# Pairwise coefficients of a delta-rule scan: from TensorE, ScalarE and GpSimd to DMAs through DRAM, with the unknown kept in PSUM and beta applied to one column at a time

## The chip, the cores and the metric

The kernel runs on one core of one Trainium2 chip. The metric is the device time of one execution in microseconds (us), the median of the runs shown. A core has five engines that run side by side and meet at semaphores: TensorE (PE, matrix products, its weight loads are listed as PEld), VectorE (DVE), ScalarE (ACT), GpSimd (POOL), and SyncE (SP), which here only issues DMAs. Each engine works through its own list of instructions in order.

## The reference, cut to what matters

The input is `x` of 4 sequences x 2048 tokens x 512 features. A gated delta-rule attention with 16 heads of 32 features comes first, then a mixture of 16 expert columns, of which one is chosen for each token. The part that the change touches is the scan over time of the attention:

```python
def step(S, inp):
    k_t, q_t, v_t, beta_t, a_t = inp
    S = S * a_t[..., None, None]
    kv_mem = jnp.einsum('bhd,bhde->bhe', k_t, S)
    delta = (v_t - kv_mem) * beta_t
    S = S + k_t[..., :, None] * delta[..., None, :]
    y_t = jnp.einsum('bhd,bhde->bhe', q_t, S)
    return (S, y_t)
```

Here `beta_t` is a vector of 32 numbers for each head, and `a_t` one number.

## The kernel before

**The chunks.** The scan isn't run token by token. Time is cut into NT = 32 tiles of T = 64 tokens, a tile into NC = 2 chunks of C = 32 tokens, and a chunk into two halves of CS = 16 tokens. Inside a chunk the deltas obey a triangular system: delta of token t is beta(t) times (v(t) - what the state gives - the sum over earlier tokens s of A(s,t) x delta(s)), where A(s,t) is k(s).k(t) times a decay. There are four such halves to a tile, written (c, j): chunk c, half j. The 64 heads-times-sequences lie as 4 groups of 32 partitions (HP = 4) times G = 16 in the free dimension.

**One half.** `solve_half` (L1206 to L1235) runs on DVE. It forms v - `uk`, where `uk` is a PSUM bank that TensorE filled with what the state (and, for the second half, the first half) contributes, and multiplies it by beta into `U` in SBUF. Then, for each of 15 tokens t0, it multiplies the row of coefficients `pairs` of t0 by column t0 of `U` (L1227) and subtracts that from the later columns (L1230). Each of these operations is cut into two (`turns`, 8 of the 16 groups each), and an operation waits for the last but one before it (`behind=1`). At the end `U` is transposed into `delT` (L1234), which TensorE wants.

**The pairs.** The coefficient of a pair (s,t) must stand on all 32 partitions of its group, and be multiplied by beta(t) of each partition. TensorE spreads it with a selection matrix `sel` (`spread_pairs`, L417, 15 products for each half, in four packs through three shared PSUM banks `work`), ACT copies each pack to SBUF (`copy_pairs`, L760), and POOL multiplies in place by beta (`pairs_times_beta`, L1015, 15 operations for each half). Row t0 of `pairs` holds its later tokens contiguous.

**A step.** A step of the main loop handles three tiles at once: `chain` (the scan of one tile), `ahead` (norm, projections q, k, gate, beta, v, and decays of the next tile) and `after` (output norm, projection, and routing to a column for the tile before). On each engine the order is written out by hand in `step(...)`. DVE's is: solve (0,0); the transposes `kd` and `decay_products(1)`; the norm of outputs; solve (0,1); first statistics of y, `add_to_state`; solve (1,0); statistics of x1, gates; solve (1,1); `decay_products(0)` for the next tile; routing (`choose_columns`, L1287 on, `rows_of_tokens`); `add_to_state`. TensorE's products between two solves are `first_half_to_u` (L437, from (c,0) to (c,1)), or `change_state` (L459), `add_to_state` on DVE (L1242) and `state_to_u` (L429).

**Semaphores that the steps below name.** `vb_free` lets ACT overwrite beta and vT with those of the next tile; DVE gives it in solve (1,1), as soon as `U` is formed. A bank of `work` goes from use to use in the order of the table `TURNS`, modulo 3; the next use waits until the bank's reader is done, and that wait is seen at L365 on PE. `xfT`, `hid`, `logits` and `rank` are uses of the routing. SP loads tokens (L300), the residual (L307) and stores the output (L312), two DMAs each per step.

**The last stage.** Behind the 33 steps (to about 4.1 ms) a loop over 80 tiles of 128 gathered tokens computes the experts. It reads weights by DMA and isn't touched, but for the names of two buffers that it borrows.

## Time and profile before

| | |
|---|---|
| time of the runs | 4683.97 us median of 3 (4678.25 to 4697.39) |
| span of the profiled execution | 4724.7 us, which is also the span of the slowest (only) core |
| its TensorE clock | 0.871 of full speed, mean |
| PE, DVE, POOL, ACT busy in it | 80%, 66%, 41%, 33% |
| DMA | 173.32 MB, 37 GB/s over the span |

The profiled execution has no time of its own in the results beside the span; the span is 0.9% above the median of the three runs. Busy shares are averages over the main loop and the last stage, which have different limits. A matmul record's end is modelled, and a fp32 product shows as two records. In a timeline a row merges neighbouring instructions of one line; its columns are start, length, engine, line, operation, out<-in, shapes, count, and in brackets the idle time before it and what ended that.

### The profile page before, as it was taken

The page shows a single profiled execution, that of the slowest core. Times are in us where ns is not written, and L with a number is a line of the kernel's source. Part 1 is how long each engine was busy: PE and PEld are TensorE (multiplying, and loading weights), DVE is VectorE, ACT ScalarE, POOL GpSimd, SP SyncE. Part 2 cuts the span into 40 slices and gives each one's busy share as a digit, 9 for nine tenths or more (in the row PEclk, how much of TensorE's full clock was granted, in tenths as well). Part 3 has the DMA queues.
Part 4 walks back from the last instruction along what each step waited for, and adds up shares of the span by engine and source line. Part 5 has one row for each costly group of instructions (what it writes and reads, how often), then busy time and mean ns, then how long its engine had stood idle before and what let it go on. Part 6 is the DMA issues. An engine that isn't in the chain of part 4 may idle for free. (4 is left out here: it accounts for less than half of the span.)

```text
span 4724.7 us, 160369 instructions
## 1 busy us (share of the span) xinstructions
PE 3787.6 (80%) x63204; PEld 2988.3 (63%) x63204; DVE 3127.4 (66%) x12284; ACT 1547.3 (33%) x2631; POOL 1924.0 (41%) x3051
## 2 busy tenths in 40 slices
PE   5888888888898888888888888888888887455553
PEld 4676676666677666676677677666667776333332
DVE  1666767766666667666766677776667667556555
ACT  2333333333333333333333333333333332211110
POOL 1343333344333333333333333334433433157776
PEclk9988989888998989988988998988899988676776
DMA  2000000000000000000000000000000000166663
GB/s 92 11 20 21 18 18 21 20 21 20 18 19 20 20 14 18 21 20 21 20 21 20 20 17 19 21 20 21 20 21 16 20 20 16 53 162 150 144 150 84
DMA packets 129486, 173.32 MB, mean 37 GB/s; under 512 B 25425, under 2 KB 67025, under 8 KB 128097
## 3 DMA queue, kind: packets, MB, share of 16 engines
q1 hardware_dynamic: 112096, 129.30, 9.7%
q0 software_dynamic: 16640, 33.71, 3.4%
q8 instruction: 510, 8.36, 0.8%
q14 instruction: 240, 1.96, 0.1%
HBM read 107.99 MB, written 59.15 MB: 35 GB/s over the span
## 5 line engine op out<-in xcount | busy, mean ns | idle before, releaser
L374 PE MATMUL work<-xT,w_sb 128*128 128x256 f32 x5120 | 1399.2, 424 | 85.3 <-PEq L365 84.5
L1015 POOL TENSOR_TENSOR pairs<-pairs,beta 128x240 f32<-128x240 f32 (+14 forms) x1920 | 802.4, 455 | 1072.1 <-POOLq L1011 1072.1
L374 PEld LDWEIGHTS work<-xT,w_sb 128*128 128x128 f32 x5120 | 1036.7, 211 | 290.8 <-issue 138.3
L1227 DVE TENSOR_TENSOR Ut<-pairs,U 128x120 f32<-128x120 f32 (+14 forms) x3840 | 917.3, 276 | 4.7
L1230 DVE TENSOR_TENSOR U<-U,Ut 128x120 f32<-128x120 f32 (+14 forms) x3840 | 877.3, 266 | 0.0
L417 PE MATMUL work<-A,sel 128*128 128x240 f32 (+14 forms) x3840 | 643.4, 318 | 118.3 <-PEq L365 118.0
L417 PEld LDWEIGHTS work<-A,sel 128*128 128x128 f32 x3840 | 592.5, 204 | 149.5 <-issue 129.3
L760 ACT ACTIVATE pairs<-work 128x480 f32<-128x480 f32 x512 | 292.5, 571 | 437.6 <-ACTq L759 436.0
L1214 DVE TENSOR_TENSOR Ut<-vT,uk 128x128 f32<-128x128 f32 x256 | 62.1, 284 | 414.1 <-DVEq L1334 230.7
L1004 POOL TENSOR_TENSOR kqd<-kq,eg 128x1024 f32<-128x1024 f32 x64 | 150.9, 2357 | 342.0 <-POOLq L1071 342.0
L384 PE MATMUL work<-qsq,squares 128*128 128x512 f32 x256 | 163.4, 725 | 125.7 <-PEq L365 125.7
L437 PEld LDWEIGHTS uk<-A,delT 16*32 16x32 f32 x8192 | 109.1, 136 | 241.2 <-issue 241.2
L437 PE MATMUL uk<-A,delT 16*32 16x16 f32 x8192 | 121.3, 201 | 148.8 <-PEq L436 146.3
L783 ACT ACTIVATE qraw<-work 128x512 f32<-128x512 f32 x128 | 76.4, 597 | 496.7 <-ACTq L782 496.7
L491 PE MATMUL work<-wo_sb,ctxT 128*128 128x512 f32 x512 | 229.2, 601 | 4.3 <-PEq L365 4.3
L729 PE MATMUL kkq<-w_sb,kq 128*128 128x512 f32 x160 | 136.7, 952 | 102.2 <-PEq L728 102.2
L709 PE MATMUL work<-squares,w_sb 128*128 128x128 f32 x320 | 71.8, 371 | 165.6 <-PEq L707 162.5
L1081 POOL DMA_INDIRECT xs_rows<-xfw,slot x64 | 64.1, 1002 | 328.3 <-POOLq L1079 318.5
L1052 POOL TENSOR_TENSOR x<-x,y 128x512 f32<-128x512 f32 x64 | 81.5, 1273 | 271.6 <-POOLq L1051 271.6
L709 PEld LDWEIGHTS work<-squares,w_sb 128*128 128x128 f32 x320 | 52.2, 193 | 214.8 <-issue 214.7
L1030 POOL TENSOR_TENSOR kd<-kd,dec 128x512 f32<-128x512 f32 x64 | 68.7, 1074 | 275.2 <-POOLq L1028 269.4
L974 ACT ACTIVATE kq<-work 128x512 f32<-128x512 f32 x80 | 47.8, 597 | 389.3 <-ACTq L972 364.9
(193 smaller groups left out, 6006.4 us busy)
## 6 DMA issues: line engine op xcount, KB each, us to landing
w_sb<-xs_rows SPq DMA_DIRECT2D x80, 258.0 KB, 2.8
w_sb<-in_w_cols SPq DMA_DIRECT2D x80, 256.0 KB, 4.4
w_sb<-in_proj_w SPq DMA_DIRECT2D x80, 256.0 KB, 4.4
xt<-in_x SPq DMA_DIRECT2D x66, 256.0 KB, 3.7
x<-in_x SPq DMA_DIRECT2D x64, 256.0 KB, 3.7
out<-x SPq DMA_DIRECT2D x64, 256.0 KB, 3.3
w_sb<-in_w_in SPq DMA_DIRECT2D x1, 5120.0 KB, 17.6
xs_rows<-w_sb SPq DMA_DIRECT2D x17, 258.0 KB, 2.6
```

The lines of the kernel that those rows point to most:

```text
L374: mm = pe.matmul(w[:, half * BT:(half + 1) * BT], w_sb[:, f, j * D + hg * P:j * D + (hg + 1) * P], xT[:, f, :], start=(f == 0), stop=(f == ...
L384: pe.matmul(w, blk1, qsq[n % 2][:], start=True, stop=True).then_inc(s["ss_full"], 1)
L417: mm = pe.matmul(w[:, o:o + n], sel[:, j * CS + t0, :], A[c][:, :, 0, j * CS + t0 + 1:(j + 1) * CS], start=(o == 0), stop=True, skip_group ...
L437: on_tiles(half, "corr_full", lambda g, q, q_half: pe.matmul(uk[q, g, CS:C], delT[c][q_half, g, :], A[c][q_half, g, 0, CS:C], start=False, ...
L491: mm = pe.matmul(w, flat(ctxT[:, hg * B + tb * BL:hg * B + (tb + 1) * BL, :]), wo_sb[:, hg, :], start=(hg == 0), stop=(hg == KD - 1))
L709: mm = pe.transpose(m_tp[u % 2][:, f * P:(f + 1) * P], xs[u][:, f * P:(f + 1) * P], ident)
L729: pe.matmul(m_yp[u % 2], hm[u % 2], pw[u], start=True, stop=True).then_inc(s["m_y"], 1)
L760: link(nc.scalar.activation(pairs[j][:, OFF[pack[0]]:OFF[pack[0]] + n], bank("pair", c, j, i)[:, 0:n], ACT.Copy))
L1004: link(nc.gpsimd.tensor_tensor(kqd[c][:], kq[:, :, c], eg[:, :, c * C:(c + 1) * C].unsqueeze(2).to_broadcast([P, G, 2, C]), ALU.mult))
L1015: ins = nc.gpsimd.tensor_tensor(a, a, beta[:, :, t:t + WID[t0]], ALU.mult)
L1227: link(v.tensor_tensor(Ut[:, g, 0:n], pr[:, g], U[:, g, at:at + 1].to_broadcast([P, G // 2, n]), ALU.mult), behind=1)
L1230: link(v.tensor_tensor(U[:, g, at + 1:at + 1 + n], U[:, g, at + 1:at + 1 + n], Ut[:, g, 0:n], ALU.subtract), behind=1)
```

## The change

The row of coefficients is now broadcast by DMA. `decay_products` writes the k part of A alone, transposed to [time, group] (`Ak`), and the q part to `Aq`. SP writes `Ak` (256 KB) to a DRAM buffer, waits until it is there, and reads it back in 8 DMAs for each half, with each row repeated on the 32 partitions of its group: 4 of 32x8x256 and 4 of 32x8x128 elements, 1.5 MB for a half, 6 MB and 0.5 MB written for a step. `pairs` now has the group index innermost. TensorE's `spread_pairs`, ACT's `copy_pairs`, POOL's `pairs_times_beta` and the 2 MB constant `sel` are gone. `U` is gone too: DVE solves in place in the PSUM bank `uk`. The pairs no longer hold beta, so each column is multiplied by its beta just before it is used (`times_beta`, 16 times two small operations for each half), and `vb_free` is given at the end of solve (1,1) and not at its beginning. SP's list is reordered round the new DMAs.

```diff
-TURNS = [("pair", 0, 1, i) for i in range(len(PACKS))] + [
...
+PIECE = CS // 2
+PIECES = [(0, 0), (PIECE, PIECE)]
+TURNS = [
+    ("xT", 0), ("xT", 1), ("qk", 0), ("rms", 0), ("alpha",), ("qk", 1), ("rms", 1), ("ss", 0),
+    ("wo", 0), ("wo", 1), ("qk", 2), ("ss", 1), ("G", 0), ("G", 1), ("qk", 3),
+    ("ss", 2), ("gate", 0), ("ss", 3), ("gate", 1), ("beta", 0), ("xfT", 0), ("xfT", 1), ("beta", 1), ("hid",),
     ("v", 0), ("logits",), ("v", 1), ("rank",)]
...
+            def fetch_pairs(c):
+                sp.wait_ge(s["Ak_ready"], 1)
+                sp.sem_inc(s["Ak_ready"], -1)
+                sp.dma_start(pair_rows[c].rearrange("h s r -> (h s) r"), Ak[c][:].rearrange("p t g -> p (t g)")).then_inc(s["rows_out"], 16)
+                sp.wait_ge(s["rows_out"], 16)
+                sp.sem_inc(s["rows_out"], -16)
+                for j in range(2):
+                    sp.wait_ge(pairs_free[j], 1)
+                    sp.sem_inc(pairs_free[j], -1)
+                    for s0, t0 in PIECES:
+                        for h in range(HP):
+                            rows = pair_rows[c, h, j * CS + s0:j * CS + s0 + PIECE, (j * CS + t0) * G:(j + 1) * CS * G]
+                            sp.dma_start(pairs[j][DH * h:DH * h + DH, s0:s0 + PIECE, t0:CS, :].rearrange("p s t g -> p s (t g)"),
+                                         rows.unsqueeze(0).to_broadcast([DH, PIECE, (CS - t0) * G])).then_inc(pairs_in[j], 16)
...
-            with sp.Fori(0, NT - 2) as i:
-                load_tokens(i + 2)
-                add_and_store(i)
...
+            with sp.Fori(0, NT - 3) as i:
+                load_residual(i)
+                fetch_pairs(1)
+                load_tokens(i + 3)
+                store(i)
+                fetch_pairs(0)
...
             def first_half_to_u(c, half):
 
                 if not half:
+                    pe.wait_ge(s["A_ready"], 1)
+                    pe.sem_inc(s["A_ready"], -1)
                     pe.wait_ge(s["delT_ready"], 1)
                     pe.sem_inc(s["delT_ready"], -1)
                 on_tiles(half, "corr_full", lambda g, q, q_half: pe.matmul(
-                    uk[q, g, CS:C], delT[c][q_half, g, :], A[c][q_half, g, 0, CS:C],
+                    uk[q, g, CS:C], delT[c][q_half, g, :], Ak[c][q_half, CS:C, g],
                     start=False, stop=True, skip_group_check=True))
...
-                link(v.tensor_tensor(A[c][:], kkq[:], dec[:, :, c * C:(c + 1) * C].unsqueeze(2).to_broadcast([P, G, 2, C]), ALU.mult))
+                d = dec[:, :, c * C:(c + 1) * C]
+                link(v.tensor_tensor(Ak[c][:].rearrange("p t g -> p g t"), kkq[:, :, 0, :], d, ALU.mult))
+                dve.sem_inc(s["Ak_ready"], 1)
+                link(v.tensor_tensor(Aq[c][:], kkq[:, :, 1, :], d, ALU.mult))
...
                 for g in turns:
-                    link(v.tensor_tensor(Ut[:, g], vT[:, g, th], uk[:, g, h], ALU.subtract), behind=1)
-                for g in turns:
-                    link(v.tensor_tensor(U[:, g, h], Ut[:, g], beta[:, g, th], ALU.mult), behind=1)
-                dve.wait_ge(s["pr_ready"], 1)
...
+                    link(v.tensor_tensor(uk[:, g, h], vT[:, g, th], uk[:, g, h], ALU.subtract), behind=1)
...
+                dve.wait_ge(pairs_in[j], 16 * HP * len(PIECES))
...
+                def times_beta(t0):
+                    at, t = j * CS + t0, c * C + j * CS + t0
+                    for g in turns:
+                        link(v.tensor_tensor(uk[:, g, at:at + 1], uk[:, g, at:at + 1], beta[:, g, t:t + 1], ALU.mult), behind=1)
 
                 for t0 in range(CS - 1):
                     n, at = WID[t0], j * CS + t0
-                    pr = pairs[j][:, OFF[t0]:OFF[t0] + G * n].rearrange("p (g t) -> p g t", g=G)
+                    times_beta(t0)
+                    pr = pairs[j][:, t0, t0 + 1:CS, :].rearrange("p t g -> p g t")
                     for g in turns:
-                        link(v.tensor_tensor(Ut[:, g, 0:n], pr[:, g], U[:, g, at:at + 1].to_broadcast([P, G // 2, n]),
+                        link(v.tensor_tensor(Ut[:, g, 0:n], pr[:, g], uk[:, g, at:at + 1].to_broadcast([P, G // 2, n]),
...
+                times_beta(CS - 1)
                 dve.wait_ge(dve_step, link.n)
-                dve.sem_inc(s["pairs_free"], 1)
-                link(v.transpose(delT[c][:], U[:]))
+                dve.sem_inc(pairs_free[j], 1)
+                if (c, j) == (NC - 1, 1):
+                    dve.sem_inc(s["vb_free"], 1)
+                link(v.transpose(delT[c][:], uk[:]))
```

On VectorE, the beginning of solve (0,1) in the first chain step read before (line, operation, out<-in, shape, repeats):

```order
L1214 TENSOR_TENSOR Ut<-vT,uk 128x128 x2
L1216 TENSOR_TENSOR U<-Ut,beta 128x8x16 x2
L1227 TENSOR_TENSOR Ut<-pairs,U 128x8x15 x2
L1230 TENSOR_TENSOR U<-U,Ut 128x8x15 x2
L1227 TENSOR_TENSOR Ut<-pairs,U 128x8x14 x2
L1230 TENSOR_TENSOR U<-U,Ut 128x8x14 x2
```

At the same place in the changed kernel (its line numbers differ):

```order
L1182 TENSOR_TENSOR uk<-vT,uk 128x8x16 x2
L1192 TENSOR_TENSOR uk<-uk,beta 128x8 x2
L1199 TENSOR_TENSOR Ut<-pairs,uk 128x8x15 x2
L1202 TENSOR_TENSOR uk<-uk,Ut 128x8x15 x2
L1192 TENSOR_TENSOR uk<-uk,beta 128x8 x2
L1199 TENSOR_TENSOR Ut<-pairs,uk 128x8x14 x2
L1202 TENSOR_TENSOR uk<-uk,Ut 128x8x14 x2
```

The multiplication of the whole half by beta has gone, and a pair of 128x8 operations stands ahead of every pair of products; each link of the chain now has `uk`, in PSUM, among its operands.

On TensorE, the end of a step and the beginning of the next read before (`su` is `change_state`, `uk` is `state_to_u`):

```order
L459 MATMUL su<-delT,kd 32x32 x32
L417 MATMUL work<-A,sel 128x240
L417 MATMUL work<-A,sel 128x224
L417 MATMUL work<-A,sel 128x16
L417 MATMUL work<-A,sel 128x208
L417 MATMUL work<-A,sel 128x192
L417 MATMUL work<-A,sel 128x80
L417 MATMUL work<-A,sel 128x176
L417 MATMUL work<-A,sel 128x160
L417 MATMUL work<-A,sel 128x144
L429 MATMUL uk<-kqd,S 32x32 x32
```

The same place now:

```order
L548 MATMUL work<-oh,squares 128x16 x2
L478 MATMUL su<-delT,kd 32x32 x32
L446 MATMUL uk<-kqd,S 32x32 x64
L420 MATMUL work<-squares,xn 128x128 x4
L469 MATMUL uq<-Aq,delT 32x32 x32
```

`state_to_u` follows `change_state` at once; the three packs of spread pairs ahead of it, and the fourth between its halves, have gone.

## Rows read from the trace of the kernel before

**Rows 1.** The page: busy time, share of the span, instructions.
```profile
PE 3787.6 (80%) x63204; PEld 2988.3 (63%) x63204; DVE 3127.4 (66%) x12284; ACT 1547.3 (33%) x2631; POOL 1924.0 (41%) x3051
```
**Rows 2.** Timeline of DVE: first solve, last step's first solve, last transpose.
```profile
116.32 0.49 DVE L1214 TENSOR_TENSOR Ut<-vT,uk 128x128 f32<-128x128 f32 x2 [15.64 <-DVEq L1334]
...
3961.55 0.48 DVE L1214 TENSOR_TENSOR Ut<-vT,uk 128x128 f32<-128x128 f32 x2 [5.57 <-DVEq L1334]
...
4039.99 0.71 DVE L1234 STREAM_TRANSPOSE delT<-U 128x512 f32<-128x512 f32 x1 [0.51 <-DVE U L1230]
```
**Rows 3.** Groups by line: busy, mean ns, idle before, releasers.
```profile
L1227 DVE TENSOR_TENSOR Ut<-pairs,U 128x120 f32<-128x120 f32 (+14 forms) x3840 | 917.3, 276 | 4.7
L417 PE MATMUL work<-A,sel 128*128 128x240 f32 (+14 forms) x3840 | 643.4, 318 | 118.3 <-PEq L365 118.0
...
L1214 DVE TENSOR_TENSOR Ut<-vT,uk 128x128 f32<-128x128 f32 x256 | 62.1, 284 | 414.1 <-DVEq L1334 230.7 <-DVEq L1349 131.4 <-DVEq L1376 40.9
```
**Rows 4.** Timeline of DVE and POOL, a solve beside POOL's multiplications.
```profile
2030.36 1.27 DVE L1227 TENSOR_TENSOR Ut<-pairs,U 128x80 f32<-128x80 f32 x2
...
2030.14 6.20 POOL L1015 TENSOR_TENSOR pairs<-pairs,beta 128x240 f32<-128x240 f32 x15 [2.23 <-POOLq L1011]
```
**Rows 5.** Timeline of DVE, a solve with POOL idle.
```profile
2050.25 0.48 DVE L1214 TENSOR_TENSOR Ut<-vT,uk 128x128 f32<-128x128 f32 x2 [0.35 <-DVEq L1395]
...
2051.29 0.48 DVE L1227 TENSOR_TENSOR Ut<-pairs,U 128x120 f32<-128x120 f32 x2
...
2059.34 0.30 DVE L1227 TENSOR_TENSOR Ut<-pairs,U 128x8 f32<-128x8 f32 x2
2059.55 0.29 DVE L1230 TENSOR_TENSOR U<-U,Ut 128x8 f32<-128x8 f32 x2
2059.98 0.71 DVE L1234 STREAM_TRANSPOSE delT<-U 128x512 f32<-128x512 f32 x1
```
**Rows 6.** Groups that compare places of operands and strides.
```profile
L1317 DVE TENSOR_TENSOR lt<-work,base 128x32 f32<-128x32 f32 x32 | 6.1, 191 | 7.6 <-DVEq L1315 7.6
L1321 DVE TENSOR_TENSOR lt<-lt,col 128x32 f32<-128x32 f32 x32 | 6.1, 191 | 4.7
...
L1463 DVE TENSOR_REDUCE A<-sel 128x80 f32<-128x1280 f32 x3 | 6.9, 2294 | 0.1
L1462 DVE TENSOR_TENSOR sel<-sel,col 128x1280 f32<-128x1280 f32 x2 | 3.0, 1492 | 0.1
...
L824 ACT ACTIVATE qr<-qr 128x512 f32<-128x512 f32 x64 | 40.3, 630 | 7.5
L834 ACT ACTIVATE vT<-work 128x512 f32<-128x512 f32 x64 | 38.2, 597 | 214.3 <-ACTq L833 214.3
```
**Rows 7.** Timeline of PE (and one row of ACT), two steps' meeting.
```profile
2061.58 3.69 PE L499 MATMUL work<-xn,gw_sb 128*128 128x256 f32 x16
...
2066.67 0.98 ACT L929 ACTIVATE ctxT<-work,gb_sb 128x256 f32<-128x256 f32 x2
...
2078.82 1.99 PE L374 MATMUL work<-xT,w_sb 128*128 128x256 f32 x8
...
2111.83 2.04 PE L384 MATMUL work<-qsq,squares 128*128 128x512 f32 x2 [4.21 <-PEq L365]
...
2114.78 3.78 PE L374 MATMUL work<-xT,w_sb 128*128 128x256 f32 x8
```
**Rows 8.** Timeline of DVE, from the state to the next solve.
```profile
2085.25 0.69 DVE L1242 TENSOR_TENSOR S<-Sd,su 128x512 f32<-128x512 f32 x1 [0.37 <-DVEq L1241]
2091.92 0.48 DVE L1214 TENSOR_TENSOR Ut<-vT,uk 128x128 f32<-128x128 f32 x2 [5.98 <-DVEq L1334]
```
**Rows 9.** DMA: queue, issues with KB and us to landing; start of DVE.
```profile
q1 hardware_dynamic: 112096, 129.30, 9.7%
...
out<-x SPq DMA_DIRECT2D x64, 256.0 KB, 3.3
...
30.83 0.48 DVE L1414 MEMSET U<- 128x512 f32 x1 [30.83 <-DMA nw<-in_norm_w]
```

More of the change, by code:

```diff
@@ L252, in sandwich_kernel @@
         m_xs, m_wc = ([sem(f"{n}{u}") for u in range(MQ)] for n in ("m_xs", "m_wc"))
+        pairs_free, pairs_in = ([sem(f"{n}{j}") for j in range(2)] for n in ("pairs_free", "pairs_in"))
         work_free = [sem(f"work{i}_free") for i in range(NW)]
@@ L751, in norm_tokens @@
                     act.sem_inc(ready, 1)
-            def copy_pairs(c, j):
-                act.wait_ge(s["pairs_free"], 1)
-                act.sem_inc(s["pairs_free"], -1)
-                for i, pack in enumerate(PACKS):
-                    n = G * sum(WID[t0] for t0 in pack)
-                    act.wait_ge(s["pair_full"], 1)
-                    act.sem_inc(s["pair_full"], -1)
-                    link(nc.scalar.activation(pairs[j][:, OFF[pack[0]]:OFF[pack[0]] + n], bank("pair", c, j, i)[:, 0:n], ACT.Copy))
-                    act.sem_inc(bank_free("pair", c, j, i), 1)
-                act.sem_inc(s["pr_copied"], 1)
             def copy_outputs(c):
@@ L1096, in _ @@
                 pool.sem_inc(f, 1)
[L1097 to L1098 removed]
+            pool.sem_inc(s["qraw_free"], 2)
+            for free in pairs_free:
+                pool.sem_inc(free, 1)
             link.restart()
```

109 lines of the change are left out of this document (29 added, 80 removed).

## The prediction

> **What bounds the kernel now.** The page comes first: PE is busy for 80% of the span, DVE for 66%, POOL for 41% [rows 1]. That would make PE the bound, but the order of the work says more. I read DVE's timeline step by step. Solve (0,0) starts 32 times, first at 116.32 and last at 3961.55 [rows 2], so a step takes (3961.55 - 116.32) / 31 = 124.0 us. The four solves of a step hang on one another through the state, and everything else of DVE stands between them. From the start of a solve (L1214) to its transpose (L1234) I find, as means over the 32 steps (128 solves, the last transpose at 4039.99 [rows 2]), 14.3 us for (0,0), 12.3 for (0,1), 16.4 for (1,0) and 9.7 for (1,1), together 52.7. The gaps behind them are 11.9, 15.3, 10.6 and 33.2 us, 71.0 together (0.3 of rounding and edges). In the gaps DVE waits for PE, but little beyond the last one: 230.7 us over 32 steps, 7.2 for each, ahead of (0,0), 4.1 ahead of (0,1), 1.3 ahead of (1,0) [rows 3]. So the step is a chain that goes from DVE to PE and back, and the change is worth what it does to the four solves and the four gaps.
>
> **The solves now.** They do the same work and yet differ by 7 us. The reader sees why where POOL multiplies the pairs: beside its 6.20 us of L1015 a DVE pair at 128x80 takes 1.27 us [rows 4], where with POOL idle one at 128x120 takes 0.48 [rows 5]. Over all its sizes L1227 takes 276 ns in the mean, nearly what L1214 takes (284), which is larger than any of them [rows 3]. The undisturbed solve runs from 2050.25 to 2059.98, 9.73 us [rows 5]. Four of these would be 38.9: 13.8 us of each step are this collision.
>
> **The solve after.** POOL's multiplications go, and DVE's operations have only one operand in SBUF beside the PSUM one. L1214, which has that form, keeps a mean of 284 ns over 256 instances [rows 3], as when nothing is beside it (0.48 for two that overlap [rows 5]). So I start from 9.73 us and take the collision as gone. Then:
> - The product with beta over the half goes: the opening two pairs and a wait take 2051.29 - 2050.25 = 1.04 us [rows 5], one pair of them 0.4: -0.4.
> - 16 pairs of 128x8 operations with beta come in, each a link that the next one waits for. The smallest links now follow at 2059.55 - 2059.34 = 0.21 us [rows 5]: 16 x 0.21 = +3.4.
> - `pairs` is read with 64 bytes from token to token. The trace has one such case: a reduction of 1280 elements read across rows takes 2294 ns, an operation on the same 1280 in order 1492 [rows 6], 0.63 ns more for each element. In the larger half of the 15 links a link costs its throughput (two operations of 120 to 64 elements, 736 for the sum of the eight sizes), so 736 x 2 x 0.63 = 0.93; in the smaller ones only one operation's latency counts, 224 x 0.63 = 0.14. Together +1.1; the other bound is 0.
> - `uk` in PSUM is read and written by every link. A DVE operation that reads PSUM takes 191 ns as one that doesn't [rows 6]. No row shows DVE writing PSUM. The nearest is ACT, where the place of an operand moves an operation by 630 - 597 = 33 ns [rows 6]. So 46 links x 33 ns = 1.5 us for a solve, up or down; I take 0, since DVE's own rows show no difference.
>
> That gives 9.73 - 0.4 + 3.4 + 1.1 = 13.8 us, with bounds of 11.2 (no stride cost, PSUM faster) and 15.3. Four solves: 55.2 against 52.7, **+2.5** for a step.
>
> The rule on strides stands in the Trainium skill too ("SBUF — State Buffer", section "Door 1: The DMA port swizzle", the note on cachelines): reads that go to a new 16-byte line each time pay a penalty. The reduction's row agrees. It gives no figure, and the sum goes by the row.
>
> **The gaps after.** (0,0) to (0,1): `decay_products(1)` becomes two operations, one more fixed part of about 0.1, and the k part is written with a stride (0 to 0.63 x 512 = 0.3): +0.3. PE isn't nearer, since it waits here for DVE's `alpha`, behind it on that list: 4.21 us idle, then at the low clock [rows 7]. **+0.3.**
>
> (0,1) to (1,0): now PE's list is full; spread pairs go from it, 643.4 / 128 = 5.0 us for each half [rows 3]. But then DVE's own work decides, which adds up to 10 us to the end of `add_to_state` (operation by operation in its timeline, of which no row is shown), and behind it PE needs 3.6 us for `state_to_u` with its projection between the halves: 13.7. And the sum of squares 1 waits for the bank that DVE frees only after its first y: that way I count 15.8 when PE is at the low clock. Between them 14.8: **-0.5.**
>
> (1,0) to (1,1): DVE's own work throughout, 10.9 in most steps: **0 to +0.3**, I take +0.2.
>
> (1,1) to (0,0): spread pairs go in front of `state_to_u`. Now 2085.94 (end of the state) to 2091.92 is 6.0 us [rows 8]; 128 small products at the low clock take 2.1 and a hop 0.2, so 2.3 is left. Over all steps the wait shrinks from 7.2 to 2.4: -4.8. But `vb_free`, until now given 0.9 us into the solve, comes at its end, 13.7 us in. Queued behind ACT's beta(0) are the copies of `xfT`, and on PE behind its bank beta(1), the outputs, `gate_hidden`, v, logits, `change_state` and `ranks`; DVE waits for those. Before, PE was past them and started `gate_hidden` 1.6 us after the transpose began (2061.58 against 2059.98 [rows 5, 7]). After, counted from the transpose: ACT and two hops 0.9, beta(1) first half at the low clock 3.8 [rows 7], outputs 1.0, second half 2.0 [rows 7], outputs 0.7, so `gate_hidden` starts at 8.3 (6.7 later). Three packs of pairs behind it go (5.0), but then the GELU, which they hid, is in the way: the hidden layer ends at 2065.3 and the GELUs at 2067.65 [rows 7], with a hop 2.6 us, against 2.0 for v's first product, so 0.7 more. The logits come 2.5 us later than now, and with them the end of the state: 28.5 us after the transpose, where it is 2085.94 - 2059.98 = 26.0 [rows 5, 8]. With 4.8 gone and 2.6 come, **-2.2.**
>
> **The DMAs.** A solve's rows are 2048 packets. The hardware queue's mean packet costs 9.7% x 16 x 4724.7 / 112096 = 65 ns of an engine [rows 9], so 2048 x 65 / 16 = 8.4 us; writing `Ak` is like a store, 3.3 us [rows 9]. From `Ak` (2 us after the transpose) the rows for (0,0) are there at about 2 + 3.5 + 2 + 8.4 = 16 us, and DVE wants them at 31; those for (0,1) at 25, wanted at 57. Those of chunk 1 have more. So I cost them at nothing, hidden by the gap of 31 us; uncovered they would cost 14 us a step. SP's list holds token loads behind the second `pairs_free`, but `xt_free` comes later still, so nothing moves. PE, ACT and POOL lose about 20, 9 and 25 us of work a step, worth nothing beyond what is said.
>
> **Once.** `sel`, 2 MB of the 10 that are loaded before DVE starts at 30.83 [rows 9], goes. At the rate of those loads (10.4 MB within some 28 us) that is -5 us.
>
> **The sum.** A step: +2.5 + 0.3 - 0.5 + 0.2 - 2.2 = +0.3 us. 32 steps: +10; once: -5; the last stage 0. So +5 on the span of 4724.7, which is 0.9% above the median of the runs; on that median, **4688 us**: no change, as large terms cancel. A difference under 0.5%, 23 us or 0.7 us a step, is about what can't be told from none here.
>
> **Rivals.**
> 1. *The stride costs nothing and the small links overlap* (or PSUM is the faster place). For it: only a reduction shows the stride's cost, no product does. 1.1 us less for a solve, 4.4 for a step: 4688 - 141 = 4547. With PSUM at its lower bound too, 4353. Chance 0.28.
> 2. *Each link through PSUM is slower.* At the upper bound of 33 ns, 6.1 us a step: 4688 + 194 = 4882. It decides from 4 ns a link on. Against it: reading costs nothing in two DVE rows. Chance 0.17. The Trainium skill ("VectorE: DVE Perf Modes", section on the TRN2 errata) has a table by which an operation with its source in PSUM takes 120 cycles where one in SBUF takes 58, at 0.96 GHz 65 ns more. By that the kernel would be near 5070. The two 191 ns rows disagree with it for reads; whether writes behave so, no row shows.
> 3. *The late `vb_free` starves PE.* If PE stays at the low clock through the whole chain behind beta(1), each of its five projections of 2.0 takes 3.8: up to 9 us, I'd say half, 4.5 a step, +144: 4832. For it: after 4.21 us idle PE ran a projection in 3.78 [rows 7]. It decides as soon as a second projection is slow. Chance 0.15.
> 4. *The rows come late.* From 25 us for a solve's rows, three times my count, DVE waits at `pairs_in`; 10 us a step would be 5000. 1.5 MB for half a solve's gap leaves much room. Chance 0.06.
>
> My forecast itself has 0.34, with a range of its own of 4620 to 4760 (a solve within 0.5 us). Faster by over 0.5%: rival 1 and a share of the forecast, 0.38. Within 0.5%: 0.2. Slower: 0.42. Low end 4520, near rival 1; the high end of 4890 takes in rival 2 at its row bound and leaves out rival 4 and the skill's figure.
>
> **What the profile after would show.** A solve of 13.8 us in all four places, with no stretched pairs; pairs of 128x8 following at 0.21; a pair of L1199 at 128x120 of 0.63 us if the stride costs, where L1227's is 0.48 [rows 5], and one of L1202 of 0.48 if PSUM doesn't. The wait ahead of (0,0) near 2.4 us, and PE idle ahead of beta(1) for 5 to 6 us, then cold. POOL busy some 1100 us, DVE above 3100. No wait at `pairs_in`. I'm wrong if a solve lies outside 13 to 14.5, or the last gap outside 30 to 32.

## The result, and the profile after

The changed kernel takes 4760.84 us (median of 4 runs, 4743.73 to 4771.22) where the kernel before, run beside it, took 4681.11 (4674.5 to 4697.39, 4 runs): a ratio of **1.0157**, 95% interval 1.0129 to 1.0185. It is slower by 1.6%, inside the forecast range, on the side that I gave 0.42, and 73 us above the predicted 4688. The narrower range that I gave my own forecast ended at 4760, just below it.

The experiments, on three chips, gave the kernel before 4701, 4724, 4728 and 4727 us, so below everything goes by the ratio to the runs of before that were taken beside them. The kernel after was run beside one set alone, the one with the lowest time of before. Whether it moves as the kernel before does from set to set isn't known, so a difference from after of less than about 1% (4728 to 4681) isn't safe, though each ratio's own interval is within 0.3% of it. The given profile of before was long for that kernel (span 4724.7); one more (label e0_before) has 4699.5.

The page of after: busy time, and two DMA queues with their packets, MB and share of the 16 engines' span.

```profile
span 4741.9 us, 153635 instructions
PE 3372.4 (71%) x59364; PEld 2518.9 (53%) x59364; DVE 3181.5 (67%) x16187; ACT 1253.7 (26%) x2119; POOL 1114.3 (23%) x1131
...
q1 hardware_dynamic: 399696, 345.37, 34.1%
...
q8 instruction: 492, 8.06, 0.8%
```

PE lost 9 points of its share and POOL 18 [rows 1], and the time rose: neither was the bound. TensorE's mean granted clock is 0.814, where it was 0.871. The groups of after:

```profile
L1199 DVE TENSOR_TENSOR Ut<-pairs,uk 128x120 f32<-128x120 f32 (+14 forms) x3840 | 827.6, 254 | 0.0
L1202 DVE TENSOR_TENSOR uk<-uk,Ut 128x120 f32<-128x120 f32 (+14 forms) x3840 | 705.4, 225 | 0.0
L1192 DVE TENSOR_TENSOR uk<-uk,beta 128x8 f32<-128x8 f32 x4096 | 606.1, 171 | 5.1 <-DVEq L1187 2.4
...
L1182 DVE TENSOR_TENSOR uk<-vT,uk 128x128 f32<-128x128 f32 x256 | 63.3, 293 | 303.7 <-DVEq L1309 123.0 <-DVEq L1324 111.5 <-DVEq L1351 58.0
```

The wait for the rows (L1187) is 2.4 us in the whole kernel, all of it in the first solve: rival 4 is out. The wait ahead of (0,0) is 123.0 us, 3.8 a step, where before had 7.2 [rows 3] and I wanted 2.4. DVE's timeline at one solve (0,0):

```profile
2099.31 0.49 DVE L1182 TENSOR_TENSOR uk<-vT,uk 128x128 f32<-128x128 f32 x2 [2.50 <-DVEq L1309]
2099.89 0.25 DVE L1192 TENSOR_TENSOR uk<-uk,beta 128x8 f32<-128x8 f32 x2
2100.10 0.62 DVE L1199 TENSOR_TENSOR Ut<-pairs,uk 128x120 f32<-128x120 f32 x2
2100.65 0.46 DVE L1202 TENSOR_TENSOR uk<-uk,Ut 128x120 f32<-128x120 f32 x2
2101.02 0.29 DVE L1192 TENSOR_TENSOR uk<-uk,beta 128x8 f32<-128x8 f32 x2
```

These are the promised signs: beta's pair with the next link 0.21 behind it, 0.62 for the pair that reads `pairs` with a stride, 0.46 for the one in PSUM. The other side of the step is PE's timeline, from the transpose of (1,1) to the product of the state. Here is a step whose last transpose starts at 2190.54:

```profile
2191.44 3.75 PE L402 MATMUL work<-xT,w_sb 128*128 128x256 f32 x8 [8.05 <-PEq L393]
...
2198.81 1.53 PE L518 MATMUL work<-xn,gw_sb 128*128 128x256 f32 x6 [0.16 <-PEq L393]
...
2215.00 0.75 PE L478 MATMUL su<-delT,kd 32*32 32x32 f32 x64
2219.68 0.53 PE L446 MATMUL uk<-kqd,S 32*32 32x32 f32 x22 [3.92 <-PEq L445]
2222.32 1.70 PE L446 MATMUL uk<-kqd,S 32*32 32x32 f32 x106 [2.11 <-issue]
```

The first four rows are nearly as worked out: PE idle ahead of beta(1) (8 us, not 5 to 6), then at the low clock (granted 0.50), `gate_hidden` at 8.3 us after the transpose. The last row isn't: after 22 of the 128 records of `state_to_u(0)` (a product shows as two) PE stands for 2.11 us with nothing to wait for ("issue"). The solve starts 33.6 us after the transpose, not 31.0.

The step by parts, in us. A line's sum differs from its step by up to 0.6, since the parts average over the first and last steps as well. "Stalls" is PE's idle time put to its own issue, over the whole run (the sum in the view of waits). The expectations quote 170 and 238 us, from a coarser count.

| kernel | solves | gaps | step | stalls | ratio to before |
|---|---|---|---|---|---|
| before, given profile | 14.3, 12.3, 16.4, 9.7 | 11.9, 15.3, 10.6, 33.2 | 124.0 | 34 | 1 |
| e0_before | 14.9, 12.3, 16.3, 9.7 | 12.0, 15.4, 10.6, 31.6 | 123.3 | 25 | 1.0001 |
| **after** | 13.6, 13.4, 13.4, 13.5 | 11.8, 15.4, 10.6, 33.3 | 125.5 | 169 | 1.0157 |
| e1_two_betas | 13.8, 13.4, 13.4, 13.7 | 11.5, 16.4, 10.7, 26.7 | 120.0 | 233 | 0.9728 |
| e2_eighth_dma | 13.5, 13.4, 13.4, 13.5 | 11.5, 15.3, 10.6, 33.9 | 125.6 | 83 | 1.0101 |
| e3_no_beta | 10.3, 10.2, 10.1, 10.2 | 10.8, 17.7, 10.6, 33.4 | 113.7 | 247 | 0.9284 |
| e4_in_order | 12.6, 12.4, 12.4, 12.5 | 10.6, 16.0, 10.6, 33.9 | 121.4 | 240 | 0.9796 |
| e5_U_in_sbuf | 16.1, 13.5, 15.8, 13.6 | 12.6, 15.9, 10.6, 34.3 | 132.8 | 171 | 1.0532 |
| e6_before_no_mul | 10.4, 11.3, 12.4, 9.7 | 9.1, 16.0, 10.6, 33.4 | 113.3 | 38 | 0.9261 |
| e7_split | 13.7, 13.4, 13.4, 13.7 | 11.9, 16.5, 10.6, 27.9 | 121.5 | 142 | 0.9785 |
| e8_betas_eighth | 13.5, 13.4, 13.4, 13.7 | 11.7, 14.8, 10.6, 23.9 | 115.4 | 108 | 0.9387 |
| e9_unrolled | 13.6, 13.4, 13.4, 13.5 | 12.0, 16.1, 10.7, 34.2 | 127.3 | 229 | 1.0143 |
| e10_rows_in_order | 12.8, 12.4, 12.4, 12.7 | 10.6, 17.8, 10.6, 29.6 | 119.3 | 410 | 0.9627 |
| e12_loop_end_moved | 12.9, 12.4, 12.4, 12.7 | 11.0, 18.2, 11.4, 26.9 | 118.2 | 471 | 0.9548 |

### The profile page after: what moved, and what is told of

The parts are those of the page before. It is cut to its first block and busy times, and to the rows that moved or that the text cites. A ratio compares the mean times of both kernels' runs of the same rounds, so it can differ in the third digit from the quotient of the medians.

```text
span 4741.9 us, 153635 instructions
## 1 busy us (share of the span) xinstructions
PE 3372.4 (71%) x59364; PEld 2518.9 (53%) x59364; DVE 3181.5 (67%) x16187; ACT 1253.7 (26%) x2119; POOL 1114.3 (23%) x1131
## 3 DMA queue, kind: packets, MB, share of 16 engines
q1 hardware_dynamic: 399696, 345.37, 34.1%
q8 instruction: 492, 8.06, 0.8%
## 5 line engine op out<-in xcount | busy, mean ns | idle before, releaser
L402 PE MATMUL work<-xT,w_sb 128*128 128x256 f32 x5120 | 1482.6, 443 | 354.9 <-PEq L393 329.2
L1199 DVE TENSOR_TENSOR Ut<-pairs,uk 128x120 f32<-128x120 f32 (+14 forms) x3840 | 827.6, 254 | 0.0
L1202 DVE TENSOR_TENSOR uk<-uk,Ut 128x120 f32<-128x120 f32 (+14 forms) x3840 | 705.4, 225 | 0.0
L1192 DVE TENSOR_TENSOR uk<-uk,beta 128x8 f32<-128x8 f32 x4096 | 606.1, 171 | 5.1 <-DVEq L1187 2.4
L1182 DVE TENSOR_TENSOR uk<-vT,uk 128x128 f32<-128x128 f32 x256 | 63.3, 293 | 303.7 <-DVEq L1309 123.0
L446 PE MATMUL uk<-kqd,S 32*32 32x32 f32 x8192 | 119.6, 215 | 161.7 <-PEq L445 121.0
L456 PEld LDWEIGHTS uk<-Ak,delT 16*32 16x32 f32 x8192 | 101.4, 127 | 211.3 <-issue 211.3
L446 PEld LDWEIGHTS uk<-kqd,S 32*32 32x32 f32 x8192 | 106.0, 127 | 189.8 <-issue 188.9
L456 PE MATMUL uk<-Ak,delT 16*32 16x16 f32 x8192 | 113.7, 197 | 127.1 <-PEq L455 127.0
L510 PEld LDWEIGHTS work<-wo_sb,ctxT 128*128 128x128 f32 x512 | 105.7, 213 | 136.0 <-issue 133.4
```

What stands on the lines that cost most here:

```text
L402: mm = pe.matmul(w[:, half * BT:(half + 1) * BT], w_sb[:, f, j * D + hg * P:j * D + (hg + 1) * P], xT[:, f, :], start=(f == 0), stop=(f == ...
L446: on_tiles(half, "uk_full", lambda g, q, q_half: pe.matmul(uk[q, g], S[q, g, :], kqd[c][q, g, 0, :], start=(g == 0), stop=True, skip_group ...
L456: on_tiles(half, "corr_full", lambda g, q, q_half: pe.matmul(uk[q, g, CS:C], delT[c][q_half, g, :], Ak[c][q_half, CS:C, g], start=False, s ...
L510: mm = pe.matmul(w, flat(ctxT[:, hg * B + tb * BL:hg * B + (tb + 1) * BL, :]), wo_sb[:, hg, :], start=(hg == 0), stop=(hg == KD - 1))
L1192: link(v.tensor_tensor(uk[:, g, at:at + 1], uk[:, g, at:at + 1], beta[:, g, t:t + 1], ALU.mult), behind=1)
L1199: link(v.tensor_tensor(Ut[:, g, 0:n], pr[:, g], uk[:, g, at:at + 1].to_broadcast([P, G // 2, n]), ALU.mult), behind=1)
```

## The experiments

**The solve, term by term.** e0_before is the kernel before again, for a second profile.

> The kernel before, unchanged, for a second profile of it. The profiled execution of before had a span of 4724.7 us where its runs took about 4681; the one of the changed kernel was its fastest run. Both theories expect a ratio of 1.00 and a span near 4680; if the span is again near 4720, profiling costs this kernel something that it doesn't cost the changed one.

Measured: ratio 1.0001 (0.9988 to 1.0014), span 4699.5, a step of 123.3 us. The last gap is 31.6 us, where the given profile had 33.2: 1.5 us of the base that I counted from were that one execution's.

> The changed kernel without the multiplications of columns by beta, which leaves beta out of the result. It prices the 16 added links. If a link of two 128x8 operations costs 0.21 us, a solve falls from 13.4 by 3.4 to 10.1 us, and a step by up to 13.4: time about 4760 - 32 x 11 = 4400, a bit less gained in the gap behind (0,1), which PE shares. The rival (links of small operations overlap, and PSUM costs the difference) expects a fall of under 2 us a solve.

```
-                    times_beta(t0)
...
-                times_beta(CS - 1)
```

Measured: ratio 0.9284 (0.9267 to 0.9301). All solves take 10.1 to 10.3 us: the 16 links of beta cost 3.3 us, where I had 3.4. They are 13 us of every step, the largest single price in the kernel.

> The kernel after, but each of the 15 products of a solve reads its rows from pairs in the order in which they lie (the same number of elements, another order of them, so the pairing of values is not the reference's). It prices the stride alone. If reading 64 bytes from token to token costs 0.6 ns an element, as the reduction of the trace before said and as the 0.61 us of the first pair of L1199 says against 0.48, a solve goes from 13.4 us to 12.4 to 12.5, the first pair to 0.48, and the kernel from 4761 to about 4640 (1.0 us x 4 solves x 31). If the stride costs nothing and the longer pair has another cause, the solve stays at 13.4 and the kernel at 4760. If the stride costs but the chain elsewhere takes it up (PE), the solve shortens and the time falls by under half of it.

```
-                    pr = pairs[j][:, t0, t0 + 1:CS, :].rearrange("p t g -> p g t")
+                    pr = (the same elements of pairs[j], taken as (g, t) in the order in which they lie)
```

Measured: ratio 0.9796 (0.9773 to 0.982), solves of 12.4 to 12.6 us. L1199 falls from a mean of 254 ns to 217:

```profile
L1199 DVE TENSOR_TENSOR Ut<-pairs,uk 128x120 f32<-128x120 f32 (+14 forms) x3840 | 691.1, 217 | 0.0
```

The stride costs 1.0 us of a solve; I had 1.1. So the stride isn't free.

> The kernel after, but with the unknown in SBUF again (a buffer U, as before), everything else as after. If the place of the unknown costs nothing by itself, the solves stay at 13.4 us and the kernel between 4740 and 4780, except where POOL works in SBUF beside a solve: there operations with two operands in SBUF can be stretched, as beside L1015 in the kernel before; POOL's remaining 1114 us mostly lie in the gaps, so I expect 0 to 1 us more for one or two of the four solves, 0 to 120 us. If PSUM costs 33 ns for each of 46 links, a solve falls to 11.9 us and the kernel to about 4580. If PSUM made it faster by itself, all four solves grow alike.

```
-                    link(v.tensor_tensor(uk[:, g, h], vT[:, g, th], uk[:, g, h], ALU.subtract), behind=1)
+                    link(v.tensor_tensor(U[:, g, h], vT[:, g, th], uk[:, g, h], ALU.subtract), behind=1)
... (and so for the products with beta, the links and the transpose)
```

Measured: ratio 1.0532 (1.0507 to 1.0557), 3.7% slower than after, more than the 120 us (2.5%) that I expected at worst. The timeline says why: (0,1) and (1,1) still take 13.5 us, as with the unknown in PSUM, so PSUM by itself costs and gives nothing that shows. But (0,0) and (1,0) take 16. Here POOL's and DVE's rows at the start of one (0,0):

```profile
1145.77 1.05 POOL L982 TENSOR_TENSOR Sd<-S,eg_end 128x512 f32<-128x512 f32 x1 [2.35 <-POOLq L981]
1145.89 1.04 DVE L1193 TENSOR_TENSOR U<-U,beta 128x8 f32<-128x8 f32 x2
...
1146.78 2.37 POOL L987 TENSOR_TENSOR kqd<-kq,eg 128x1024 f32<-128x1024 f32 x1
...
1146.89 2.67 DVE L1200 TENSOR_TENSOR Ut<-pairs,U 128x120 f32<-128x120 f32 x2
```

A pair of 0.62 us takes 2.67, 0.3 more than POOL's product beside it, and beta's of 0.25 takes 1.04. With one operand in PSUM no L1199 of after is above 0.37 us. The Trainium skill ("SBUF — State Buffer", section "SBUF: two separate sides") states this as an exclusive lock on a port pair between GpSimd and a VectorE operation with two operands in SBUF, held for the whole instruction; by that rule DVE's pair can't end before POOL's product has, and the trace agrees: 1149.56 us against 1149.15.

> The kernel before without POOL's 15 products of a half's pairs with beta (beta is left out of the coupling of the pairs; PE's spread, ACT's copies and all else stay). It prices the collision of POOL with DVE alone. If POOL's products are what made the solves unequal, all four take 9.7 us, 38.9 for a step in place of 53.3, and the solves give 14 us a step; if DVE's chain still set the end the kernel would take about 4240. PE's list is still full (80% busy before, about 118 us a step at the clocks that it got), so I expect it to give back part of this in the gaps: 4350 to 4500, a step of 112 to 117 us. If POOL was not the cause, the solves stay unequal and the time near 4680.

```
-                for t0 in range(CS - 1):
-                    ... ins = nc.gpsimd.tensor_tensor(a, a, beta[:, :, t:t + WID[t0]], ALU.mult)
-                ins.then_inc(s["pr_ready"], 1)
+                pool.sem_inc(s["pr_ready"], 1)
```

Measured: ratio 0.9261 (0.9237 to 0.9285). The solves sum to 43.8 us, not to 38.9: POOL's products of pairs made 9.5 us of the collision against e0_before, and the 4.9 that are left fall where POOL's other products run: beside (0,0) the decay of k and q, beside (0,1) the gate, beside (1,0) the decays of the state; beside (1,1) POOL runs nothing, and it takes 9.7 us. My "13.8 us are this collision" was nearly right in sum and wrong in whom it named. The change takes away both, the first by dropping the products, the second by moving the unknown to PSUM.

**The last gap.**

> The changed kernel with two buffers for beta, used in turn; the semaphore vb_free, which now only guards vT, is given after the first two operations of solve (1,1), and ACT waits for it ahead of vT and not ahead of beta. Theory 1 (the loss is the late release of beta): PE's idle time of 8.1 us ahead of the second beta projection goes, and the gap from solve (1,1) to (0,0) falls from 33.3 us by 5 to 7: 4760 - 32 x 6 = about 4570, below both kernels. Theory 2 (the gap is set by what PE does behind that, or by PE's instructions coming late): the gap falls by less than 2 us, the time stays above 4700.

```
-        beta = sb("beta", [P, G, T])
+        beta = [sb(f"beta{p}", [P, G, T]) for p in range(2)]
... (ACT writes beta[1 - p] without a wait; vb_free, now for vT alone, is given at the solve's start)
```

Measured: ratio **0.9728** (0.9708 to 0.9748), 4.2% faster than after and 2.7% than before. The last gap falls by 6.6 us, near the 6.7 by which I had put `gate_hidden` later. So the late `vb_free` has its full price once the packs no longer stand beside it.

> The changed kernel, each read of pairs fetching one row of its eight: the same 16 DMAs a chunk with an eighth of the bytes and packets. What isn't fetched stays zero (a memset of pairs on POOL before the first step), so the pair terms of most tokens are left out. Theory 2: within runs of small products PE waited 170 us for nothing that the profile shows (issue), where before it was 34; if that is PE's instructions fetched behind the pair rows on the same 16 DMA engines, the 170 fall below 50 and the time falls by 40 to 110 us, to 4650 to 4720. Theory 1 (the loss is in the order of the semaphores): nothing changes, 4745 to 4775. Solves stay at 13.4 us in both.

```
-                            rows = pair_rows[c, h, j * CS + s0:j * CS + s0 + PIECE, ...]
+                            rows = pair_rows[c, h, j * CS + s0:j * CS + s0 + 1, ...]
```

Measured: ratio 1.0101 (1.0082 to 1.012). PE's stalls fall from 169 to 83 us, not below 50, and the time by only 0.55%, which is within the 1% that isn't safe. The last gap is even 0.6 us longer: in 28 of 31 steps a second projection behind the transpose runs near the low clock (granted 0.53):

```profile
2208.05 3.54 PE L402 MATMUL work<-xT,w_sb 128*128 128x256 f32 x8
```

After has this in 10 of 31 steps (su later by 2.3 us). Why it comes in some steps and not in others I can't say: the idle time ahead of beta(1) is 7.0 to 9.4 us in both kernels.

> The kernel with two betas (4572.6 us, 238 us of PE idle with nothing but its own issue in the records) with PE's bursts of 128 to 192 small products broken by larger ones: a transposition of xn between the halves of the state's product with the keys, an output projection between the halves of the state's product with the queries, a gate projection between the halves of the chunk's outputs. If PE stalls because a long burst of small products uses up its instructions faster than they come, the idle time of that kind falls from 238 to under 120 us, the last gap of a step from 26.7 to about 25, and the kernel to 4500 to 4550. If the stalls come from the transfers of the pairs alone, whatever PE runs, their sum stays above 180 us and the kernel stays within 0.5% of 4573, or gets 0.5 us a step slower by the transposition that now stands in the state's way.

```
 state_to_u(0, 0); [xT turned, half]; state_to_u(0, 1)
 state_to_outputs(0, 0); output_projection(0); state_to_outputs(0, 1); output_projection(1)
 project("gate", 4, 0, 0); chunk_to_outputs(0, 0); project("gate", 4, 0, 1); chunk_to_outputs(0, 1)
```

Measured: ratio 0.9785 (0.9761 to 0.9809). The stalls fell from 233 to 142 us, and the kernel became 0.6% slower: the ones that went gave no time back, and `state_to_u` now waits for the transpositions. Neither forecast of the stalls was met (under 120, above 180); as an account of the time, the theory of bursts alone fell. But the list of gaps showed what to look at: they alternate (26.2, 31.0, 26.3, 32.0), and the long ones are those in which the loops over two steps end, PE's and DVE's.

> The kernel with two betas, with one row in eight of the pairs' rows transferred (the others of pairs stay zero, so part of the coupling between tokens is left out). In the kernel with two betas every second step has the loop's end of PE behind change_state, at 15.2 us after the last transpose of a step; PE goes on with state_to_u only at 24.6 us although the state is ready at 18.5, and stands again for 3 us after 22 products, while the rows of (0,0) travel. In the kernel after, the same place comes at 25.2 us, when the rows are there, and costs 6.6 to 7 us in all. If the transfers hold up PE's instructions, the loop's end costs 7 us here too, so the last gap of those steps falls from 30 to 25 or 26 us and that of the others from 25 to about 23: 3 to 4 us a step in the mean, a ratio to the kernel before of 0.950 to 0.958 where the two betas alone had 0.973. If they don't, both gaps and the time stay (0.970 to 0.976).

The edit is that of e1 and e2 together. Measured: ratio **0.9387** (0.9374 to 0.94), 3.5% below the two betas alone, against the 0.55% that the same edit gave to after, and below the 0.950 to 0.958 that I expected: the last gap fell by 2.8 us, as forecast, and the second by 1.6 as well. The place where PE's loop ends, in e1_two_betas:

```profile
2116.45 0.75 PE L478 MATMUL su<-delT,kd 32*32 32x32 f32 x64
2126.34 0.54 PE L446 MATMUL uk<-kqd,S 32*32 32x32 f32 x22 [9.13 <-PEq L445]
2129.16 1.07 PE L446 MATMUL uk<-kqd,S 32*32 32x32 f32 x63 [2.29 <-issue]
```

and in e8_betas_eighth:

```profile
2041.63 0.75 PE L478 MATMUL su<-delT,kd 32*32 32x32 f32 x64
2046.25 0.54 PE L446 MATMUL uk<-kqd,S 32*32 32x32 f32 x22 [3.86 <-PEq L445]
2049.22 1.70 PE L446 MATMUL uk<-kqd,S 32*32 32x32 f32 x106 [2.43 <-issue]
```

In the first, DVE's timeline shows that the state was ready at 2120.87, 5.5 us before PE went on:

```profile
2120.18 0.69 DVE L1218 TENSOR_TENSOR S<-Sd,su 128x512 f32<-128x512 f32 x1 [0.37 <-DVEq L1217]
```

A view of busy time by window shows what else ran; its last three columns are the granted clock, the DMA engines' share and GB/s:

```profile
2117.00:2126.00 9.00, 0.20 (x24) 0.09 (x10) 2.74 (x13) 1.62 (x2) 2.00 (x2) 0.69 0.99 206
```

While PE stood, the DMA engines were full (0.99), mostly with the rows of (0,0) (in the DMA view of 2117 to 2126.3 queue q1 has 76.6% of their time, the scatter of tokens by POOL, q0, 17.0%). With an eighth of the rows the 9.13 become 3.86, here the plain wait for the state. In after this place comes 10 us later, when the rows are there, which fits the little that the edit gave it.

That PE waited for its instructions can be seen more directly, for the trace has the branch and the packets that carry instructions. PE's branch at the end of its loop, in after, e1_two_betas and e8_betas_eighth (duration in ns, least, median and most; the 76 is the last turn, which doesn't jump back):

```profile
L694 PEldq COMPARE_BRANCH  x15: 76/3477/3775, 458.2 to 3980.0; - x15
L694 PEldq COMPARE_BRANCH  x15: 76/8993/9448, 427.3 to 3809.2; - x15
L694 PEldq COMPARE_BRANCH  x15: 76/3968/4527, 417.3 to 3666.2; - x15
```

The queue q8 moves instructions in packets of 16 KB (492 in after), q14 mostly in packets of 8 KB. The trace doesn't name the engine that a packet is for; that q8 serves PE and q14 DVE is read from the times here and below. PE's branch above begins at 2117.05. In the DMA view of 2117.1 to 2121.4 no packet of q8 starts (first two rows; a packet's whole time is put to the window in which it starts, hence the 119%), and in that of 2121.4 to 2126.4 two do (last row):

```profile
q1 hardware_dynamic: 1360, 0.85, 119.0%
q14 instruction: 1, 0.01, 1.0%
...
q8 instruction: 2, 0.03, 3.2%
```

The second starts at 2123.31 and lands at 2124.59; the branch ends 1.38 us behind that. In after the packet behind which the branch ends starts 0.94 to 1.09 us behind the branch's own start, at each of the 14 that jump back, in e1_two_betas 4.0 to 6.6 us, in e8_betas_eighth 1.0 to 2.0; a packet itself takes 1.1 to 1.2 us (median) in all of them. So what the rows cost is the wait until the packet starts. The same holds for the stalls put to issue: of those over 1 us, 70 of 72 in after, 92 of 94 in e1_two_betas and all 37 in e8_betas_eighth end 1.1 to 1.7 us behind the landing of a packet of q8; of times picked at random 7 or 8% do.

> The kernel after with the loops of PE, ACT, POOL and DVE over the steps written out three times (5 turns of 6 steps instead of 15 of 2). In the kernel after, each end of PE's loop (every second step) leaves PE standing for 2.5 to 2.9 us after the first 22 products of state_to_u. If the loop's end is what those stalls come from, 10 of 15 go: the last gap of these steps comes to 31.0 to 33.5 us like that of the others, about 27 us in all, a ratio to the kernel before of 1.008 to 1.011 where after had 1.016. If long bursts of small products stall wherever they stand, or the loop's end costs something only because of the transfers, the stalls stay and the ratio stays at 1.013 to 1.019.

```
-            with pe.Fori(0, NT // 2 - 1):
-                step(1, True, True, True)
-                step(0, True, True, True)
+            with pe.Fori(0, (NT // 2 - 1) // 3):
+                for _ in range(3): ... (both steps; the same for ACT, POOL and DVE)
```

Measured: ratio 1.0143 (1.0127 to 1.0158), not told apart from after. In 10 of 14 places the stall behind 22 records is gone, but other stalls come (0.39 us twice in most `state_to_u(0)`, up to 2.6 within `change_state`), 229 us in all, and a last gap without a loop's end or another disturbance takes 32.6 to 32.8 us where after had 30.9 to 31.3. Of the stalls over 1 us, 68 of 69 again end 1.1 to 1.7 us behind a packet of instructions. What hinders PE is the late instruction, of which the loop's end is only one occasion; why these steps have it here and not in after, no run shows.

> The kernel with two betas, with A kept by halves (half, column, token), so that the rows in DRAM and in pairs lie in the order in which DVE reads them and one source of 8 KB goes to each partition in one piece, a third more bytes in far fewer pieces. It undoes the stride: a solve should go from 13.4 to 13.8 us to 12.3 to 12.6, 4 us a step, 120 us in all: a ratio of 0.946 to 0.950 where the two betas alone had 0.973. If the larger pieces also free the way for PE's instructions, the gaps shrink too and the ratio is 0.930 to 0.940; if the added third of bytes holds PE up more, or the shorter solves are given back in the gaps as PE's own list is full, it is 0.955 to 0.970.

```
-        Ak = [sb(f"Ak{c}", [P, C, G]) for c in range(NC)]
+        Ak = [sb(f"Ak{c}", [P, 2, G, CS]) for c in range(NC)]
-        pairs = [sb(f"pairs{j}", [P, CS, CS, G]) for j in range(2)]
+        pairs = [sb(f"pairs{j}", [P, CS, G, CS]) for j in range(2)]
+                        rows = pair_rows[c, j, h * C + j * CS:h * C + (j + 1) * CS, :].rearrange("s r -> (s r)")
```

Measured: ratio **0.9627** (0.9606 to 0.9647), 1.0% better than the two betas alone where the solves alone are worth 3%. Each solve gained its 1.0 us. The gaps took 3.3 of the 4 back: the second is 1.4 longer, the last 2.9, the first 0.9 shorter. There are a third more bytes of rows (412.45 MB on the queue against 345.37), and the stalls rise to 410 us. That the pieces are larger (153936 packets against 399696) didn't help. Bytes and size of pieces changed together, so which of them holds PE up longer isn't shown.

> The kernel with two betas and rows in order (ratio 0.963 to the kernel before), with the end of PE's loop over the steps moved from ahead of state_to_u(0) to behind the third sum of squares, in solve (1,0): there 24 projection products stand behind it, PE has 4 to 5 us of idle time ahead of first_half_to_u(1), and no rows travel. Every second last gap was 33.3 us where the others had 25 to 29.5 (mean 28). If the loop's end, with PE's instructions late while the rows of (0,0) travel, is what lengthens it, those 15 gaps come to about 28: 5 us x 15 = 75 us, a ratio of 0.945 to 0.949, and the idle time of PE at that place disappears. If the stall comes with the burst of 128 small products and the transfers, wherever the loop ends, the gaps stay near 30 or more in the mean and the ratio is above 0.957. A new stall of over 5 us ahead of first_half_to_u(1) would show that the loop's end costs as much there.

```
+            step(1, True, True, True)             # up to the third sum of squares
+            with pe.Fori(0, NT // 2 - 2):
+                rest(1, True, True, True)
+                whole(0, True, True, True)
+                step(1, True, True, True)
```

Measured: ratio **0.9548** (0.9535 to 0.9561), the best version with all of the work in it: 4.5% faster than before and 6.0% than after. The last gap falls by 2.8 us; 1.6 come back in the other three, more than I expected. The new place costs 4.06 and 1.46 us of PE in one step, in the first half of solve (1,0), which hides most of it.

The forecast was met neither in the ratio nor in its pattern, for the gaps still alternate: the long ones fell from 33.5 to 29.9 us in the mean and the others from 27.4 to 24.9. In the long ones PE now ends `state_to_u(0)` 25.3 us behind the transpose, where in e10 it was 33.3: 8.0 us are won on PE. But DVE's own loop ends in the same gap, and now DVE is the late one. Its branch is at 2093.76; PE's product is done at 2097.21:

```profile
2095.91 1.30 PE L445 MATMUL uk<-kqd,S 32*32 32x32 f32 x76 [0.30 <-issue]
2102.20 0.49 DVE L1194 TENSOR_TENSOR uk<-vT,uk 128x128 f32<-128x128 f32 x2 [8.84 <-DVEq L1322]
```

DVE's next instruction of any kind comes at 2101.98, 1.62 us behind the landing of a packet of 8 KB on q14. In after DVE goes on 2.8 to 3.2 us behind its branch, in e12 6.6 to 8.4, and in all 14 of these gaps the solve starts 3.0 to 5.3 us behind PE's last product, where it is 0.15 to 0.17 everywhere else. That is 62 us of this kernel, and every one of the 14 resumes 1.6 to 1.7 us behind a packet of q14. Moving PE's loop end alone uncovered the next one; moving DVE's too, into its wait for PE, wasn't tried.

Elsewhere the rows still hold PE up, worst here, in the middle of a burst and with no loop near:

```profile
2124.11 0.98 PE L463 MATMUL uq<-kqd,S 32*32 32x32 f32 x92
2133.09 0.75 PE L463 MATMUL uq<-kqd,S 32*32 32x32 f32 x36 [8.00 <-issue]
```

and the same 8 us in the view by window, with the DMA engines at 0.73:

```profile
2125.00:2133.00 8.00, 0.09 (x10) 0.00 (x0) 8.00 (x60) 0.01 (x1) 1.68 (x2) 0.60 0.73 152
```

The only packet of q8 in this time starts at 2130.30, 5.2 us behind PE's stop, and lands 1.41 us before PE goes on.

## Why the prediction was right where it was, and where it failed

- **The solve: right.** 13.4 to 13.6 us in all four places against 13.8. From 9.7: -0.4, +3.3 (had 3.4), +1.0 (1.1), PSUM 0 (0). Four of them take 53.9, not 55.2. The base of 9.73 us was right as well, though the collision taken away is only to two thirds the one named (e6).
- **The first three gaps: right within 0.6.** 11.8, 15.4 and 10.6 against 12.2, 14.8 and 10.8.
- **The last gap: the step that failed.** "Over all steps the wait shrinks from 7.2 to 2.4: -4.8", and "-2.2" for the gap: 31.0 was forecast, 33.3 measured, outside the 30 to 32 that I had named as the bounds of being right; 2.3 us of every step, 71 us of the kernel. The 9 steps of after without any disturbance have 30.9 to 31.3, so the chain that I counted is right. What I left out is what comes on top of it in the others, by their timelines:
  - 14 of 31 steps have the end of PE's loop: 1.8 to 2.9 us of stall within `state_to_u(0)`, 32 us in all, each ending behind a packet of instructions;
  - 10 have a second projection at the low clock, 2.3 us each, 23 us. That is rival 3, at a sixth of the price that I gave it (144);
  - 4 stand for 2.3 to 2.6 us within `change_state`, with its followers at the low clock; the last `su` product ends 4.2 us later, 17 us in all.
  
  The loop's end had cost before too (its gaps alternate between 29.9 and 34.2 in the mean in e0_before). I had read one step of before and subtracted means over all of them: in the step that I read, the wait ahead of (0,0) was 5.98 us [rows 8] and not 7.2, so the same chain gives -3.6 and +2.6, that is -1.0 and not -2.2. That is 1.2 us of the 2.3; the rest is what the disturbances of after have more than those of before.
- **The base, and luck.** The sum stood against a profile whose last gap was 1.5 us longer than in e0_before. Against that one a step is 2.2 us longer (125.5 to 123.3): 0.6 from the solves (53.9 to 53.3) and 1.7 from the last gap, less 0.2 in the first. The 71 us of the last gap and the 73 us by which the total is off only look alike. Between the two given profiles the kernel lost 17 us (4741.9 against 4724.7) where I had +5: the 71 were mostly set off by solves 1.3 us shorter than forecast (43 us) and by the start and end (23). The other 60 us of the miss are about the distance of each profile from its median: before's span lies 41 us above the median of its three runs, and after's profile is of its fastest run, 19 below the median. So that the total fell inside the range says little of the last gap.
- **The DMAs: half right.** They are in time for DVE, as forecast. That they cost nothing was wrong where they meet PE's and DVE's instructions; in after itself this is little (e2: 0.55%, not safe), in a tighter schedule much (e8: 3.5%).
- **Once: undersized.** The first solve starts at 96.14 us, 20 earlier than before [rows 2], against the 5 that I gave; and from the last transpose (4064.69) to the end it is 677 us where it was 685. These 28 us (20 and 8) hide part of the 45 that the steps lost against the given profile (3890.0 us from the first solve (0,0) to the last, where it was 3845.2).
- **Rivals.** 1 (stride free, small links overlapping) fell by e4 and e3, 2 (PSUM slower) by e5, 4 by the 2.4 us of L1187. The 65 ns that the Trainium skill has for a source in PSUM didn't show (e5); the estimate from it, 5070, is 310 us off.

How far is this shown? That PE and DVE stand for late instructions is shown by the branches and packets above, and that the rows make them later by e1 against e8, in runs with two betas. How the 2.3 us of after itself divide is read off its timelines: e2 and e9 each took something away there, and the last gap grew (33.9 and 34.2), since more steps had a cold projection in the one and the stalls came elsewhere in the other. The second cold projection stays open; no run took it away alone.

## What to carry to other kernels

When work moves from an engine to DMAs, look not only at whether the data come in time, but at who is starved while they travel: an engine that runs many short instructions needs its own instructions in that time, and the worst place is a loop's end on the critical path, of any engine that the chain passes through. When a semaphore is given later (here `vb_free`, which one more buffer avoids), price it without the cover of the work that the same change removes: it was worth 4.2%. And take a base for a chain from steps of the same kind; a mean over alternating steps hides a cost that will stay.

## What the runs showed of the hardware

- PE's instructions and the kernel's transfers compete. PE's branch at the loop's end took 3.5 us (median) in after, 9.0 with the rows of (0,0) under way and 4.0 with one row in eight; in the middle of a burst PE stood 8.00 us with the DMA engines at 0.73. The page counts instructions among the DMA traffic (q8, 8.06 MB), and PE went on 1.1 to 1.7 us behind such a packet's landing in 70 of its 72 stalls of over 1 us. The Trainium skill ("Runtime: NRT & Kernel Launch", section "Instruction fetch mechanics") says that a sequencer fetches its instructions over a DMA queue of its own, and that a taken branch to a target outside the pages at hand forces a fetch before the engine can go on; the runs agree. It also calls the cost of crossing from one block to the next in straight code mostly hidden, and here the runs don't agree: PE's stalls, most of them in straight code, sum to 83 to 471 us in after and its variants, against 25 to 38 in before and its own.
- DVE's loop end, which costs nothing while PE is later, took 2.8 to 3.2 us in after, and 6.6 to 8.4 in e12, where it delayed 14 solves by 3.0 to 5.3 us.
- In after, behind the end of its loop, PE always ran just 22 records (11 products) and stood again, for 1.8 to 2.9 us, and as long with an eighth of the rows (1.9 to 2.7 in e2).
- A VectorE pair with both operands in SBUF took 2.67 us instead of 0.62 beside a GpSimd product of 2.37 us; with one operand in PSUM none was stretched. Keeping the unknown in PSUM was worth 3.7% of this kernel (e5).
